# Earlier loads of B, C and delta on SyncE's queue in a Mamba, attention and gated-recurrence kernel

## What is computed

```python
h  = layernorm(layernorm(x))                    # x and h both kept
xz = rmsnorm(h) @ in_proj_w;  xi, z = split(xz)
xc = silu(causal_conv4(xi) + conv_b)
dbc = xc @ x_proj_w                             # dt (64), B (16), C (16)
delta = softplus(dbc[..., :64] @ dt_proj_w + dt_proj_b)
# for each feature e and state n, over the 512 tokens t:
#   state[t] = exp(delta[t] * A) * state[t-1] + (delta*xc)[t] * B[t]
#   y[t]     = sum over n of state[t] * C[t]  +  D_param * xc[t]
out = (y * silu(z)) @ out_proj_w
```

## Time and profile before

| | us |
|---|---|
| median of 3 runs | 1724.57 |
| lowest and highest | 1723.18, 1725.14 |
| profiled execution, its own time | 1722.45 |
| profiled execution, span | 1720.6 |
| TensorE busy | 1392.9 (81%) |
| VectorE busy | 1165.9 (68%) |
| ScalarE busy | 885.4 (51%) |
| GpSimd busy | 696.3 (40%) |
| first phase ends about | 790 |

### The profile page before, as it was taken

One profiled execution on the slowest core, in us unless ns is written; L12 is line 12 of the kernel. 1 busy time (PEld: TensorE's weight loads), 2 busy tenths in 40 slices (PEclk: granted clock), 3 DMA queues, 4 the chain that ended last, 5 costly groups with the idle time before them and its releaser, 6 DMA issues. The chain is left out here.

```text
span 1720.6 us, 17276 instructions
## 1 busy us (share of the span) xinstructions
PE 1392.9 (81%) x5520; PEld 659.7 (38%) x5520; DVE 1165.9 (68%) x1819; ACT 885.4 (51%) x1512; POOL 696.3 (40%) x407
## 2 busy tenths in 40 slices
PE   2332677979798989899973889999999999999994
PEld 1100343545444454545531223434443434343432
DVE  1296978978887888883125787676767667666325
ACT  3545456657574847453210465556555554645533
POOL 3466777859595967671313221212112121200000
PEclk9666788989999999999985799999999999999997
DMA  4424124151515151601035332423332332320034
GB/s 150 156 72 161 61 91 155 54 179 39 207 40 196 37 195 35 190 25 37 13 90 130 75 84 67 99 63 92 69 82 69 88 74 63 75 62 2 27 115 153
DMA packets 93785, 158.03 MB, mean 92 GB/s; under 512 B 8592, under 2 KB 74704, under 8 KB 90576
## 3 DMA queue, kind: packets, MB, share of 16 engines
q1 hardware_dynamic: 93696, 156.94, 30.8%
HBM read 110.91 MB, written 46.01 MB: 91 GB/s over the span
## 5 line engine op out<-in xcount | busy, mean ns | idle before, releaser
L1232 DVE TENSOR_REDUCE mx<-psum 128x1 f32<-128x512 f32 x512 | 345.4, 687 | 210.3 <-PE psum L1717 208.1
L1483 ACT ACTIVATE pw<-psum 128x512 f32<-128x512 f32 x512 | 300.2, 597 | 317.1 <-PE psum L1732 316.1
L868 POOL TENSOR_TENSOR hb<-ddb,bcb 128x1024 f32<-128x1024 f32 x128 | 304.9, 2403 | 128.4 <-DMA ddb<-dd 82.5
L503 DVE TENSOR_TENSOR_SCAN psum<-psum,hb 128x512 f32<-128x512 f32 x224 | 261.6, 1213 | 81.0 <-POOL hb L868 73.4
L1717 PE MATMUL psum<-kp,qp 96*128 96x512 bf16 x512 | 204.8, 401 | 45.8 <-DVE mx L1232 24.9
L694 ACT ACTIVATE psum<-ddb,A_neg 128x512 f32<-128x512 f32 x256 | 165.5, 680 | 132.7 <-DVE hb L506 68.8
L1732 PE MATMUL psum<-qp,kp 99*128 99x512 bf16 x512 | 197.5, 387 | 7.3 <-ACT pw L1483 6.0
L1625 POOL TENSOR_TENSOR rstd<-rstd,neg_half 128x4 f32<-128x4 f32 x16 | 16.3, 1019 | 410.8 <-DVE rstd L1217 410.8
L1743 PE MATMUL psum<-pw,v_sb 128*32 128x512 f32 x1024 | 138.1, 611 | 3.6 <-DVE ot L1256 2.3
L506 DVE TENSOR_TENSOR hb<-psum,bcb 128x1024 f32<-128x1024 f32 x112 | 137.2, 1225 | 3.9
L928 PE MATMUL psum<-back,w 128*128 128x512 f32 x256 | 115.3, 605 | 8.3 <-ACT back L710 8.3
(11 more groups left out here) (184 smaller groups left out, 2165.4 us busy)
## 6 DMA issues: line engine op xcount, KB each, us to landing
ddb<-dd SPq DMA_DIRECT2D x64, 512.0 KB, 8.9
bcb<-bc SPq DMA_DIRECT2D x32, 512.0 KB, 7.8
parts<-parts_sb SPq DMA_DIRECT2D x96, 128.0 KB
dd<-dd_out SPq DMA_DIRECT2D x8, 1024.0 KB, 4.0
qp<-parts SPq DMA_DIRECT2D x32, 256.0 KB, 7.7
kp<-parts SPq DMA_DIRECT2D x16, 384.0 KB, 4.6
x_front<-x_dram SPq DMA_DIRECT2D x8, 512.0 KB, 3.9
xh<-x_front SPq DMA_DIRECT2D x8, 512.0 KB, 2.9
```

The lines of the kernel that those rows point to most:

```text
L503: e.tensor_tensor_scan(to[:, g, :], a[:, g, :], h[:, g, :], 0.0, ALU.mult, ALU.add).then_inc(scan_ok, 1)
L868: e.tensor_tensor(hb[n % NHB], ddb[k % NSLOT][:, 1:2, :].to_broadcast([P, 2, L]), bcb[q][:, 0, :, :], ALU.mult).then_inc(bx_ok, 1)
L1232: used.up(e.tensor_reduce(mx[u % 2][:, n:n + 1], bank(used.n % 2), AXIS.X, ALU.max))
L1483: e.activation(pw[n % NPW], bank(5 + n % 2), ACT.Exp, scale=HD ** -0.5).then_inc(exp_ok, 1)
```

## The change

In `sp_first` the loads of the next block move. Before, with each turn, the first pair `bc_load(i + 1, 0)` and the delta loads 0 and 1 were issued after delta's transfer, `xh` and the load of `x_front`; the second pair and loads 2 to 5 came at the head of the next turn. Now the first pair and loads 0 to 3 stand directly behind delta's transfer, in front of `xh`. Loads 4 and 5 and the second pair stay at the head of the next turn. For block 0 both pairs are issued before delta's transfer, right behind that of B and C.

```diff
                 if s:
-                    bc_load(i, 1)
-                    for j in range(2, 6):
+                    if i > 0:
+                        bc_load(i, 1)
+                    for j in range(4, 6):
                         dd_load(i, j)
...
+                if i == -1:
+                    bc_load(0, 0)
+                    bc_load(0, 1)
                 if mid:
                     b = i + 1
                     e.wait_ge(du_ok, b + 1)
...
                     e.dma_start(dd_dram[b % 2].rearrange("(f p) c t -> p f c t", p=P), dd_out).then_inc(dd_sent, 16)
+                    if b > 0:
+                        bc_load(b, 0)
+                    for j in range(4):
+                        dd_load(b, j)
                 if front:
...
-                if mid:
-                    bc_load(i + 1, 0)
-                    dd_load(i + 1, 0)
-                    dd_load(i + 1, 1)
                 if back:
```

## The result

The changed kernel takes 1669.51 us (median of 4 runs, 1669.16 to 1670.08) where the kernel before, with one run more than above, has 1724.38 (1723.18 to 1725.14). The ratio is 0.9683, with a 95% interval of 0.9666 to 0.97. The profiled execution took 1669.34 us, its span is 1667.5 against 1720.6. The second phase, from the last `xc` to the end of the span, is 931.6 us long before and 930.6 after, so all but 1 us was gained in the first phase.

What follows compares the result with a forecast made beforehand. VectorE's first scans were taken to wait for GpSimd's product, held by delta's loads queued behind `xh`. 8.1 + 10.1 + 10.7 + 20.6 + 7.6 = 57.1 us off 1724.6 gave 1667.5, said as 1668; range 1661 to 1689.

Steps and rivals of the forecast that it cites:

- The load leaves the path: Blocks 1 to 7: delta's loads land 6.5 us after issue; in block 3 4.9 us before GpSimd is free.
- the late rival: Delta's loads take up to 13.9 us to land, 15.7 us lost: 1683; chance 0.24 shared with slow clock.
- Block 0, 8.1: Block 0's first scan moves from 84.40 to 76.3, when ScalarE's first exponential ends: 8.1 us.
- Blocks 1 and 2, 20.8 together: `w_out` moves up to the end of `w_in` and gets shorter: 10.1 and 10.7 us.
- What is late next, blocks 3 to 6: First scans then wait for ScalarE's exponential; 0.2 us of idle time stays in each block, gain 20.6 us.
- The sum as worked: All terms together, 57.1 us, giving 1668; the case 1661 to 1674 had chance 0.70.
- `w_out` at the full clock, 7.6: Blocks 3 to 6: behind a gap of 1.0 us `w_out` takes 3.72 us, not 6.60; 1.9 us per block.
- The slow-clock rival: `w_out` stays at 6.6 us, so the gain is 44.2 us: 1680; chance 0.24 shared with late loads.
- Little more than this sum can be had: From block 3's `w_out` to the next `w_in`'s end, TensorE fits the new block time with 2 us to spare.
- What is delayed, price 0: `xh` and `x_front`'s load go out later, but 34 us of cover before VectorE reads `x_front` makes it cost 0.
- change its name: Rival: loads 2 or 3 hold SyncE, or something unseen ends with VectorE; nothing moves, 1724.6; chance 0.04.
- the slower side: Rival: `x_front` lands past 382 and VectorE stands at `front_moments` in blocks 0 to 5; chance 0.02.

Runs made afterwards that it cites:

- run with GpSimd's wait: Changed kernel plus one added wait: from block 3 on GpSimd starts unit 1's product only when VectorE has updated `c_state`; 1665.16 us, ratio 0.9654.
- GpSimd's wait and the filler in the last two turns: Changed kernel plus GpSimd's wait for `c_state` from block 3, and unused matmuls (12 and 4) before the last two `w_out` products; 1658.22 us, ratio 0.9626.
- with two loads ahead: Changed kernel with only delta's loads 0 and 1 in front of `xh`, loads 2 and 3 at the head of the next turn; 1678.43 us, ratio 0.9727.

## Why the prediction came out right, and where its steps did not

**The load leaves the path: right.** GpSimd's wait for `ddb` nearly vanishes, the wait for `hb` is 12.3 us (13 forecast). Of the seven waits for it at first scans only 0.89 us in block 2 is left. Over all blocks a `ddb` load now lands 3.4 to 10.0 us after issue, median 6.7, close to the 6.5 that was taken from block 7; the late rival's 13.9 did not occur.

**Block 0, 8.1: right, 8.7 measured.** ScalarE's exponential is the limit, as said. From the issue of delta's transfer to the first scan it was 18.3 us and is 10.3, in the changed kernel and in the four kernels of the experiments that keep its block 0: 8.0 us. The rest is chance: delta's transfer went out 0.7 us earlier than in the trace before (65.42 and 66.09), and between 65.2 and 67.7 in the runs here.

**Blocks 1 and 2, 20.8 together: right, 19.9 measured.** `w_out` follows `w_in` without a gap and takes 3.62 us. The 19.9 are the 33.6 us at block 3's first scan less block 0's 8.7 and block 3's own 5.93 − 0.97 = 5.0; the 0.97 is explained in the next step.

**What is late next, blocks 3 to 6: the step that failed in size.** The prediction kept 0.2 us of the idle time in each, for ScalarE's exponential, and took VectorE free at 346.8 for granted, since it was free then in the trace before. But it was free then *because GpSimd stood still*: the 7.86 us of idle time in the earlier trace rows lay beside the update of `c_state`. With the load early, the products move in beside it, and the update takes 2.19 to 2.62 us in blocks 3 to 6 instead of 1.22. That is 1.0 + 3 × 1.4 = 5.2 us, less the 4 × 0.2 = 0.8 that it hides: 4.4 us. The run with GpSimd's wait gives 3.9 of them back between the first scans of blocks 2 and 6. The trace before had the sign of it, in the one block where GpSimd does not stand still. The prediction took its landing of 6.5 us from block 7, and the update of `c_state` there reads 2.02 us, where the updates of blocks 3 to 6 have 1.22 or 1.23:

```profile
707.48 2.02 DVE L557 SCALAR_TENSOR_TENSOR c_state<-c_state,late 128x1024 f32<-128x1024 f32 x1
```

In block 5, in the changed kernel:

```profile
485.27 2.61 DVE L561 SCALAR_TENSOR_TENSOR c_state<-c_state,late 128x1024 f32<-128x1024 f32 x1
487.80 2.33 DVE L507 TENSOR_TENSOR_SCAN psum<-psum,hb 128x512 f32<-128x512 f32 x2
```

The sum as worked fits a kernel without that overlap: at block 6's first scan it has 55.2 us, the run with GpSimd's wait 56.3 (623.57 − 567.29), the changed kernel 51.4. By the last `xc` they are 59.6 (788.97 − 729.42) and 52.0, where 57.1 was forecast; the wait's run gains more than the sum because block 7's update, long already in the trace before, is short in it too.

**`w_out` at the full clock, 7.6: right in kind, one block short.** Blocks 3 to 5 have 3.72 us as taken; block 6 has 5.41, and gains 0.6 us (85.84 − 85.22) where 1.9 was forecast; a fast one would have given 1.5 more. The gap was put at 1.0 us and is 1.63 to 2.05, because of the same late scan. With GpSimd's wait the gap is 0.97 us and all of blocks 3 to 6 are fast. The slow-clock rival was wrong in five of six blocks.

**"Little more than this sum can be had": wrong.** It looked only at TensorE's chain from block to block. GpSimd's wait and the filler in the last two turns together take another 0.6% (0.9626 after 0.9683), some 10 us. The prediction said that block 7 gets nothing, which is true of the change; that its `w_out` still idles 6.57 us before it could have been read as an opening.

**What is delayed, price 0: right.** `xh` takes 6.1 us to land in block 3 (5.8 forecast, 343.5 − 337.66) and 4.1 to 8.8 in the other blocks, and the cover of 34 us was tested above.

**The other rivals.** The wait did not change its name one for one, loads 2 and 3 did not hold SyncE until the block ended (the four issues took 4.03 us), and nothing on the slower side showed.

The total: 57.1 forecast, 54.9 us between the medians, 53.1 between the spans. The spans' difference is made up so: 57.1 less 4.4 (stretched updates), less 1.3 (slow `w_out` in block 6), less 0.9 (blocks 1 and 2), plus 0.6 (block 0) and 1.0 (second phase) gives 52.1, which leaves 1.0 us unexplained; it stands in blocks 3 to 6. That 1668 came within 1.5 us of the measured 1669.51 is in part luck: the mechanism's own shortfall is 4.0 us between the profiles, and 1.8 of them do not show in the medians, since the profiled execution before happened to be 1.9 us faster than its median.

## What to carry to other kernels

On a queue in which a wait holds all behind it, look for loads whose data is ready while the queue stands in front of something they don't need, and price the landing from a place in the same trace that already has the new order. When a wait is removed, the engine that waited begins to work beside something else: ask which of the neighbour's instructions now run beside it, and whether they kept their length in the trace only because it stood still. A wait added in front of work that nobody needs yet can make the program faster, here by 4.4 us. When a gain falls short, compare the lengths of the same instructions in the two traces before any theory on waits.

## What the runs showed of the hardware

**VectorE's instructions stretch beside GpSimd's products, but only some.** Those with two inputs in SBUF can: `c_state<-c_state,late` goes from 1.22 to as much as 2.62 us, and with two loads ahead a convolution step from 0.75 to 2.71 us (three of them 6.18) and the product `dd_out<-dd_out,middle` of line 497 from 1.21 to 3.36. They don't each time; most convolution steps keep 0.75. Those with one input in PSUM do not, in the same stretches: the scan pair stays at 2.31 to 2.35 us, and all 112 products with C in the changed kernel take 1.22 to 1.23, as this one during GpSimd's four products:

```profile
313.74 1.23 DVE L510 TENSOR_TENSOR hb<-psum,bcb 128x1024 f32<-128x1024 f32 x1
```

GpSimd pays too: those four took 10.30 us, where four in a row without such a neighbour took 9.28. The Trainium skill ("SBUF — State Buffer", "SBUF: two separate sides") says that a VectorE instruction with two SBUF inputs and a GpSimd one that reads SBUF take turns whole, whoever starts first. By that rule, as an estimate, the worst stretch is one whole product, 2.35 us; the 1.40, 1.96 and 2.15 us measured (2.62 − 1.22, 2.71 − 0.75, 3.36 − 1.21) stay below it, and the sparing of the scans agrees. It was not tried whether the operand's place alone decides.

**Gaps of 2 us before `w_out` don't settle its clock.** In blocks 4, 5 and 6 of the changed kernel the same instructions stand in front, the gap is 2.04, 2.05 and 2.05 us, and `w_out` takes 3.72, 3.72 and 5.41 us, with a granted clock of 1.00, 1.00 and 0.68. Over the nine kernels here, gaps of 2.00 to 2.05 us were followed by a fast `w_out` six times and by a slow one three times, each time in block 6. Behind 1.78 us or less it was fast every time; behind 2.27 us in the last turn, where the narrow matmuls of the sums stand in front instead of `w_in`, and behind 3.81 us or more, slow every time. The product with `uo` at the start of the second phase, behind 2.74 us, was fast (3.72 us) in six of the nine and slow (5.3 to 5.4) in three. Between 1.78 and 3.81 us a kernel should not count on either.

**A transfer behind four broadcast loads** of 512 KB lands later: `xh` took 6.1 us in block 3 and, in block 0, 8.8 (issued at 71.93), where it was 2.9 before in both. In the kernel with only block 0 changed it took 8.0 in block 0 and 2.9 in blocks 1 to 5.
